# First heads stored and loaded first over two queues, terms interleaved, and the bias fold moved to the last batch

## What is computed

```python
h = _layernorm(x) * (1 + ca) + sa          # sa, ca, ga ... from silu(c) @ wmod
Q, K, V = heads(Wq, bq), heads(Wk, bk), heads(Wv, bv)      # 16 heads of 8
scores = Q K' / sqrt(8) + lambda * (tanh(Q) J) tanh(K)'    # causal
x = x + ga * (softmax(scores) V @ Wo.T + bo)
h = _layernorm(x) * (1 + cb) + sb
expert = argmax(h @ centroids.T)           # 8 experts, one for each row
xn = (h - mu) * rsqrt(var + EPS) * gamma_e + beta_e
y = h + relu(xn @ W1_e.T + b1_e) @ W2_e.T + b2_e
x = x + gb * (alpha * y + (1 - alpha) * h)
```

## Time and profile before

| | |
|---|---|
| median of 3 runs | 775.23 us |
| the profiled execution's own time | 773.26 us |
| its span in the trace | 771.5 us |
| TensorE busy | 676.7 us (88%) |
| VectorE busy | 545.0 us (71%) |
| ScalarE busy | 500.7 us (65%) |
| GpSimd busy | 258.0 us (33%) |

### The profile page before, as it was taken

How to read it: one execution, slowest core, us unless ns; L and a number is a source line. 1 busy time by engine, 2 the same in 40 slices (tenths; PEclk the granted TensorE clock), 3 DMA queues, 4 the chain that set the end, 5 groups by cost and what they waited for, 6 DMA issues and landing times.

```text
span 771.5 us, 15278 instructions
## 1 busy us (share of the span) xinstructions
PE 676.7 (88%) x5199; PEld 341.3 (44%) x5199; DVE 545.0 (71%) x1249; ACT 500.7 (65%) x1182; POOL 258.0 (33%) x342
## 2 busy tenths in 40 slices
PE   3657899999999998999999989999998989887693
PEld 2352344333333433433344434343443227886593
DVE  6959666887866786778667868788777603897352
ACT  1431577766767866766877586866767788655472
POOL 2009109200201943513138234210352202466443
PEclk9867699999999999999999999999999999999797
DMA  8996732456533251925606165636313445424610
GB/s 224 316 206 240 131 68 64 131 98 113 118 67 60 71 178 32 177 56 148 124 1 193 58 112 97 157 94 129 97 43 112 161 142 169 126 78 146 177 40 11
DMA packets 55572, 91.88 MB, mean 119 GB/s; under 512 B 10257, under 2 KB 26157, under 8 KB 55240
## 3 DMA queue, kind: packets, MB, share of 16 engines
q1 hardware_dynamic: 49308, 79.72, 41.6%
q0 software_dynamic: 3520, 8.42, 3.1%
q10 hardware_dynamic: 2668, 2.78, 1.3%
HBM read 51.04 MB, written 37.90 MB: 115 GB/s over the span
## 4 chain that ended last, share of the span: by engine, by line
PE 54%; DVE 20%; ACT 12%; issue 7%; DMA 4%; another core or an unknown queue 1%; ACTq 1%; DVEq 0%; POOL 0%; SPq 0%; POOLq 0%
PE PS L1232 15%; PE PS L1192 12%; PE PS L1258 11%; ACT arenaA L1014 7%; DVE PS L1672 6%; PE PS L1309 4%; PE PS L1320 3%; DVE block_max L1679 3%; ACT arenaB L932 2%; PE PS L1262 2%; DVE arenaA L1355 2%; DVE arenaB L1355 2%; PE PS L1197 1%; PE PS L1140 1%
## 5 line engine op out<-in xcount | busy, mean ns | idle before, releaser
L1014 ACT ACTIVATE arenaA<-PS 128x512 f32<-128x512 f32 (+3 forms) x768 | 332.4, 498 | 157.3 <-PE PS L1262 119.9
L1672 DVE CUSTOM_DVE_ANT_0 PS<-PS,mask 128x1024 f32<-128x1024 f32 (+3 forms) x256 | 261.4, 1035 | 90.4 <-PE PS L1192 85.4
L1258 PE MATMUL PS<-arenaA 99*128 99x512 bf16 (+3 forms) x768 | 221.5, 332 | 14.9 <-ACT arenaA L1014 11.6
L1192 PE MATMUL PS<-arenaA 96*128 96x512 bf16 (+3 forms) x768 | 198.8, 335 | 26.0 <-DVE maxima L1672 8.2
L1258 PEld LDWEIGHTS PS<-arenaA 99*128 99x128 bf16 x768 | 71.6, 97 | 202.5 <-ACT arenaA L1014 141.6
L1232 PE MATMUL PS<-arenaA,Vs 128*9 128x512 f32 (+3 forms) x1536 | 158.3, 488 | 0.0
L1679 DVE TENSOR_REDUCE block_max<-PS 128x8 f32<-128x1024 f32 (+1 forms) x96 | 100.4, 1045 | 28.8 <-PE PS L1197 26.1
L1192 PEld LDWEIGHTS PS<-arenaA 96*128 96x128 bf16 x768 | 66.7, 100 | 90.9 <-DVE maxima L1672 31.3
L1262 PE MATMUL PS<-after,identb 128*128 128x128 bf16 x512 | 104.5, 221 | 0.0
L1063 ACT ACTIVATE arenaA<-PS,b1p 128x128 f32<-128x128 f32 x184 | 52.6, 374 | 35.3 <-PE PS L1309 21.2
L831 POOL DMA_INDIRECT out_dram<-arenaA x46 | 46.1, 1002 | 82.7 <-DVE arenaA L1355 73.8
(11 more groups left out here) (219 smaller groups left out, 691.1 us busy)
## 6 DMA issues: line engine op xcount, KB each, us to landing
arenaA<-k_parts SPq DMA_DIRECT2D x96, 128.0 KB, 8.0
arenaA<-by_expert SPq DMA_DIRECT2D x46, 192.5 KB
o_raw<-OT SPq DMA_DIRECT2D x32, 256.0 KB, 2.1
k_parts<-arenaB SPq DMA_DIRECT2D x24, 256.0 KB, 3.8
arenaA<-q_parts SPq DMA_DIRECT2D x16, 384.0 KB, 5.2
q_parts<-arenaB SPq DMA_DIRECT2D x18, 256.0 KB, 3.8
arenaA<-in_L_ffn_W_dram SPq DMA_DIRECT2D x2, 2048.0 KB, 12.9
arenaA<-q_parts SPq DMA_DIRECT2D x16, 256.0 KB, 5.7
```

The source lines that it names most:

```text
L1014: a.activation(PT[:, u % EB, h, off:HALF], PS[:, 4 + n % SB_, off:HALF], ACT.Exp).then_inc(exp_ok, 1)
L1192: last = mm(PS[:, place + c0 // HALF, at:at + c1 - c0], SQ(g, h)[0:KROWS, t * P:(t + 1) * P], SK(g, h)[0:KROWS, c0:c1], start=(at == 0), s ...
L1258: last = mm(bank[:, off:HALF], SK(g, h)[0:MROWS, kb * P:(kb + 1) * P], SQ(g, h)[0:MROWS, qc * HALF + off:(qc + 1) * HALF], start=True, sto ...
L1672: v.tensor_tensor_reduce(out=src, in0=src, in1=mask[:, S - n:S], scale=1.0, scalar=-3e38, op0=ALU.add, op1=ALU.max, accum_out=maxima[:, pl ...
```

## The change

- **Stores.** `store_first` writes only the first group's 4 heads (64 KB each instead of 256 KB): K's on SyncE, Q's on ScalarE's queue. The other 12 heads (192 KB, all 12 of them on SyncE) follow after the loads of group 0.
- **Loads.** The rows of the six terms become neighbours: row r of term t is now row 6r + t of the stack (`t:KROWS:TERMS`) instead of 16t + r. Queries take 6 transfers of 128 KB as the keys do; a group takes 12 instead of 9. Group 0's queries are issued half by SyncE, half by ScalarE.
- **W2** is loaded after group 0's loads instead of at the start, and its eight turns begin after maximum 13 of group 0 instead of right behind W1's.
- **Order on SyncE.** The values, then a wait for all parts, then group 1; the first maxima are sent between the two stores of turned weights.
- **Fold.** Beta and a second copy of W1 (2 MB in 4 pieces) are loaded in the last body's group 1, into the free part of arena B; b2 with them. GpSimd folds right after its last sends; ScalarE waits for `b1_ok` before `hidden` instead of before attention.

```diff
+            queue.dma_start(stacks[t:KROWS:TERMS, g, side, :, :],
+                            (q_parts, k_parts)[side][bass.ds(b, 1), g * HG:(g + 1) * HG, PART_OF[side][t], :, :].rearrange("a h r q -> (a r) h q"))\
+                .then_inc(stack_in[g], 16)
...
+        FIRST_HEADS = ((0, HG), (HG, H))
+
+        def store_first(queue, n, heads, done):
+
+            k, dst, off = TENSORS[n]
+            h0, h1 = heads
+            for j in range(3):
+                queue.dma_start(dst[0, h0:h1, j, off:off + HD, :], T16[h0 * HD:h1 * HD, k, j, :]).then_inc(done, 16)
...
-            sp.wait_ge(parts0_k, PARTS_OUT // 2)
+                store_first(sp, n, FIRST_HEADS[0], first_k_out)
+            sp.wait_ge(first_k_out, PARTS_OUT // 2)
             load_side(0, 0, 1)
-            sp.wait_ge(parts0_q, PARTS_OUT // 2)
-            load_side(0, 0, 0)
+            sp.wait_ge(first_q_out, PARTS_OUT // 2)
+            for t in (0, 2, 4):
+                load_term(sp, 0, 0, 0, t)
+            sp.dma_start(Aap[:, 20480:24576].rearrange("p (e f) -> p e f", e=E), W2.rearrange("e d n -> d e n")).then_inc(w2_in, 16)
+            for n in (1, 2):
+                store_first(sp, n, FIRST_HEADS[1], parts0_k)
+            for n in (0, 3):
+                store_first(sp, n, FIRST_HEADS[1], parts0_q)
             sp.wait_ge(va_ok, 1)
             load_values(0)
+            sp.wait_ge(parts0_k, PARTS_OUT // 2)
+            sp.wait_ge(parts0_q, PARTS_OUT // 2)
             load_group(0, 1)
...
-            send_maxima(0, T_FIRST)
+                if k == 0:
+                    send_maxima(0, T_FIRST)
...
+                    sp.wait_ge(pv_ok, group * NU + EB + 5 + k)
+                    some = slice(k * E // W_PARTS, (k + 1) * E // W_PARTS)
+                    sp.dma_start(W1F[:, k * E * FC // W_PARTS:(k + 1) * E * FC // W_PARTS, :].rearrange("p (e c) d -> p e (c d)", c=FC),
+                                 W1[some].rearrange("e (p c) d -> p e (c d)", c=FC)).then_inc(fold_in, 16)
+                sp.dma_start(BETA, every(beta)).then_inc(fold_in, 16)
+                sp.dma_start(b2_b[:, :], every(b2)).then_inc(b2_in, 16)
...
+                    if body == "last" and g == 1:
+                        load_fold(b * NG + g)
...
-            pool.wait_ge(b1_ok, 1)
+            pool.wait_ge(b1_in, 16)
...
             send_rows(B - 2, (B - 1) * NG + 2)
+            fold_beta()
...
+                store_first(act, n, FIRST_HEADS[0], first_q_out)
+            act.wait_ge(first_q_out, PARTS_OUT // 2)
+            for t in (1, 3, 5):
+                load_term(act, 0, 0, 0, t)
...
-                for _ in range(6 if i == len(PREP) - 1 else 1 if i >= len(PREP) and turned_weights < 16 else 0):
+                for _ in range(6 if i == len(PREP) - 1 else 1 if i >= len(PREP) + (0 if turned_weights < 8 else W2_FROM) and turned_weights < 16 else 0):
```

More of the change, by code:

```diff
@@ L402, in _ @@
             sp.dma_start(W1r.rearrange("p (e c) d -> p e (c d)", e=E), W1.rearrange("e (p c) d -> p e (c d)", c=FC)).then_inc(w1_in, 16)
-            sp.dma_start(Aap[:, 20480:24576].rearrange("p (e f) -> p e f", e=E), W2.rearrange("e d n -> d e n")).then_inc(w2_in, 16)
-            Q_ROWS = ((0, 0, 3), (3, 0, 2), (5, 0, 1))
-            K_ROWS = ((0, 0, 1), (1, 0, 1), (2, 0, 1), (3, 1, 1), (4, 1, 1), (5, 2, 1))
             def load_side(b, g, side):
-                src, terms = ((q_parts, Q_ROWS), (k_parts, K_ROWS))[side]
-                for t, j, n in terms:
-                    sp.dma_start(stacks[t * ROW:(t + n) * ROW, g, side, :, :],
-                                 src[bass.ds(b, 1), g * HG:(g + 1) * HG, j:j + n, :, :].rearrange("a h j r q -> (a j r) h q"))\
-                        .then_inc(stack_in[g], 16)
+                for t in range(TERMS):
+                    load_term(sp, b, g, side, t)
             def load_group(b, g):
@@ L500, in load_reciprocals, with load_fold @@
                     .then_inc(num_in, 16)
+            def load_fold(group):
+                every = lambda v: v.rearrange("e d -> (e d)").rearrange("(a n) -> a n", a=1).to_broadcast([P, E * D])
+                for g in range(NG):
+                    sp.wait_ge(values_in[g], B * 16)
+                for k in range(W_PARTS):
+                    sp.wait_ge(pv_ok, group * NU + EB + 5 + k)
[4 more added lines that the diff above has]
+                sp.dma_start(b2_b[:, :], every(b2)).then_inc(b2_in, 16)
             def attention(b, body):
@@ L846, in _ @@
             act.dma_start(lam_c[:, :], row(lam).to_broadcast([P, 1])).then_inc(bias_in, 16)
-            act.dma_start(b2_b[:, :], row(b2.rearrange("e d -> (e d)")).to_broadcast([P, E * D])).then_inc(bias_in, 16)
             act.dma_start(b1c[:, :, :], b1.rearrange("e (p c) -> p e c", c=FC)).then_inc(b1_in, 16)
-            act.dma_start(OT[:, :, :].rearrange("p a q -> p (a q)"), row(beta.rearrange("e d -> (e d)")).to_broadcast([P, E * D])).then_inc(beta_in, 16)
             act.wait_ge(cols_ok, 1)
@@ L976, in _ @@
             for n in (0, 3):
-                k, dst, off = TENSORS[n]
                 act.wait_ge(split0_ok, POS0[n] + 1)
-                for j in range(3):
-                    act.dma_start(dst[0, :, j, off:off + HD, :], T16[:, k, j, :]).then_inc(parts0_q, 16)
+                store_first(act, n, FIRST_HEADS[0], first_q_out)
+            act.wait_ge(first_q_out, PARTS_OUT // 2)
+            for t in (1, 3, 5):
+                load_term(act, 0, 0, 0, t)
             for k in range(16):
@@ L1054, in _ @@
             attention(B - 1, "last")
+            act.wait_ge(b1_ok, 1)
             def hidden(n):
@@ L1184, in maximum @@
                 if k == 0:
-                    pe.wait_ge(stack_in[g], (loads + 1) * 9 * 16)
+                    pe.wait_ge(stack_in[g], (loads + 1) * 12 * 16)
                 n = (t + 1) * P
@@ L1793, in _ @@
             last_table = tile_table(1)
+            dve.wait_ge(b2_in, 16)
             for n in range(TURNS):
```

35 lines of the change are left out of this document (18 added, 17 removed).

## The result

The changed kernel takes 776.57 us (median of 16 runs, 773.78 to 778.68), the kernel before beside it on the same chip 774.12 (16 runs). The ratio is 1.003, 95% interval 1.0019 to 1.004: slower by 0.3%, where 770.5 and a gain were predicted. Against the 774.12 measured beside it, the forecast of -4.7 would have been 769.4; it came out at +2.45. One of the 16 runs of the kernel before took 872.41 us, a slow one that the ratio leaves out. The profiled execution took 776.91 us, with a span of 775.1 where it was 771.5.

A forecast was written before the change was run, and what follows sets the result against it. Bound: in setup a chain through Q's last store and group 0's query load, then VectorE. Terms -6.2 + 0 + 0 + 0 + 1.5 = -4.7 from the median of 775.23 gave 770.5 us; range 765.5 to 775.5.

The forecast's parts named there:

- Part 1: Setup, group 0's stacks: first maximum on TensorE moves from 51.78 to 45.6, -6.2 us (bounds -6.6 to +0.3).
- I take 41.3, nearer the low end: Setup: landing time of Q's last first store, chosen between bounds of 40.3 and 45.0 us.
- A quarter of the bytes lands no sooner: Rival, setup: smaller stores on four DMA engines land at 43.9; first maximum -3.6, total -2.1, 773.1 us; chance 0.15.
- ScalarE's "nothing, with 0.2 to spare": Setup: ScalarE's stores and loads before W1's evacuations last to about 42.6; turn 5 ready at 43.3, due 43.5.
- Part 2: Stretch of maxima in setup, W2's eight turns moved behind maximum 13: 0 us (bounds +3.5 to -2.3).
- Half clock at all turns: Rival, stretch of maxima: all eight W2 turns at half clock, +3.5 us, 774; chance 0.05.
- Part 3: Group 1's stack, loaded behind the landed parts, is in by 64 to 67, due at 70.0: 0 us.
- the slower rival: Group 1 late: its loads in at 75 to 78, TensorE waits 5 to 8 us, 777.5 to 779.5; chance 0.08.
- Part 4: Three more transfers per group load, some 21 us of SyncE in all, covered by its waits: 0 us.
- Part 5: Moved fold 0; its loads delay group 14's maxima rows, +1.5 us (bounds 0 to +5).

The follow-up runs named there:

- fold_only: The kernel before with only the change's bias fold (W1 loaded again, beta and b2 in the last body, fold behind the last scatter); ratio 1.0082.
- b2_behind_maxima: The changed kernel with b2's rows alone issued behind group 14's maxima, beta's still ahead of them; ratio to the kernel before 0.9997.
- rows_behind_maxima: The changed kernel with the rows of beta and b2 issued behind group 14's maxima; 768.75 us beside the kernel before's 770.98, ratio 0.9971.
- setup_only: The kernel before with the changes to setup and the row terms, its fold kept at the start; 769.8 us beside 770.98, ratio 0.9986.
- split_without_terms: The kernel before with setup's part of the change, but the stacks' loads in their old form and the old fold; 772.86 us beside 770.82, ratio 1.0021.
- row_terms_only: The kernel before with only the form of the stacks' loads changed (12 per group); 770.69 us, ratio 0.9943; repeated 767.82, 0.9961.
- w2_turned_early: rows_behind_maxima with W2 loaded and turned right behind W1, first maxima sent behind both stores of turned weights; ratio to the kernel before 0.9963.
- terms_and_flat: row_terms_only with the parts reordered in DRAM, all 16 heads in one store of 128 plain rows; ratio to the kernel before 0.9964.
- flat_stores: rows_behind_maxima with the parts reordered in DRAM, so each store is one evenly spaced run of rows; 767.96 us, ratio 0.9913; repeated 764.16, 0.9903.
- flat_split_old_fold: flat_stores with the fold at the start, as in the kernel before; ratio to the kernel before 0.9952; repeated 766.4 us, 0.994.
- store_probe: The changed kernel with eight extra unread stores in the middle bodies; next transfer issued 3.37 and 3.19 us behind 4x8 stores, 3.93 and 3.14 behind 16x8.

## Why the prediction was wrong, by its steps

Two milestones carry most of it. In one table from the profiled executions: VectorE's first maximum, from there to the issue of the first rows, and from the issue of group 14's rows to the evacuation behind it.

| kernel | first maximum | to first rows | at group 14 |
|---|---|---|---|
| before | 52.66 | 27.76 | 10.45 |
| changed, two profiles | 50.55, 51.18 | 29.11, 28.44 | 15.08, 15.72 |
| fold_only | 52.60 | 28.35 | 15.35 |
| b2_behind_maxima | 52.07 | 29.39 | 11.35 |
| rows_behind_maxima | 50.33 | 27.79 | 11.26 |
| setup_only | 51.25 | 29.23 | 10.45 |
| split_without_terms | 53.17 | 28.44 | 10.44 |
| row_terms_only, two | 49.98, 50.39 | 28.80, 27.77 | 10.46, 10.46 |
| w2_turned_early | 49.69 | 28.74 | 10.44 |
| terms_and_flat | 49.32 | 28.81 | 11.25 |
| flat_stores, two | 47.84, 47.55 | 28.45, 28.44 | 10.45, 10.45 |
| flat_split_old_fold, two | 47.84, 47.35 | 26.56, 28.25 | 10.45, 10.45 |

**Part 1, -6.2: measured -2.1, and by another mechanism.** "I take 41.3, nearer the low end" is the step that failed. It let a store shrink with its bytes; the 4x8 pattern kept it at 5.55 us, and the stores landed at 43.62. The two terms behind it were mis-sized as well: the last of three loads was issued 1.5 us later (45.14) where 0.9 was added, and landed in 4.40 where 3.4 was. These are 2.3 + 0.6 + 1.0 of the 4.1 us that were missing. The first is the rival *A quarter of the bytes lands no sooner*, which had the landing right (43.9) but its -3.6 too large by the other two, and got 0.15. I had seen the shape that decides it in the order of instructions. Nor are the 2.1 us due to the stores: row_terms_only gains 2.7 without them (2.3 when repeated), and split_without_terms, with them, is 0.5 later than the kernel before. I had counted the loads' new form only at the end of the path, as 3.4 instead of 5.76 us (4.40 was measured, and 2.62 in row_terms_only), and overlooked that the keys' loads, in the same form, get out of the way of Q's stores.

**ScalarE's "nothing, with 0.2 to spare"**: it hung on the 41.3 and the spare failed with it: ScalarE began 4.65 us later than before, and TensorE stood 2.87. Since the loads landed later still, it cost nothing. In flat_stores, where the stores land at 40.5, ScalarE is at its turns by 42.73 and TensorE doesn't stand, as Part 1 had it.

**Part 2, 0: measured +1.35 and +0.7** in the two profiles. The clock was not full between the first maxima but at 0.50 for 18 us, up to the second of W2's late turns; the other six ran at full clock, so the rival *Half clock at all turns* didn't happen. (Its +3.5 was no exact sum either: 8 turns of 0.4 are 3.2.) Part of the +1.35 is chance, since rows_behind_maxima is the same program up to there and took 27.79, with its clock up at 0.95 between 55 and 60. 1.05 us came back between the first rows and attention's first evacuation. Of these, 0.65 lie before attention's first score products on TensorE, 3.80 us behind the rows' issue before (84.22, after a wait of 0.44 for the rows) and 3.15 here (82.81, after none); the rest isn't traced.

**Part 3, 0**: right. No chunk of group 1 waited for a stack; the slower rival did not happen. (By its own waits of 5 to 8 us it would have ended at 778.5, not 779.5.) **Part 4, 0**: right, and more: the twelve shorter transfers are the one part that gains.

**Part 5, the fold 0, its loads +1.5: measured +4.6.** The mechanism was right, also the slack of nothing, and TensorE's wait of 2.67 us lies in the bounds of 0 to 5. Two things failed. The queueing was mis-sized: the rows landed 6.2 us after their issue, where I had added 1.5 to 3.56, and that 1.5 counts from the end of the issue (580.7 is 2.2 behind its start at 578.50). And the sum had no term for the clock, though the earlier trace rows had shown it fall in setup. Once TensorE stood, the clock fell to 0.50, and the other 1.96 of the 4.6 us were lost behind the wait. In three more profiles with both loads ahead of the rows, waits of 2.62 us (fold_only), 3.37 (store_probe) and 3.78 (the changed kernel again) were followed by a clock of 0.50 and a further 2.3, 1.1 and 1.5 us.

**The sum.** -2.1 + 1.35 - 1.05 - 0.65 (group 12) + 4.63 = +2.2 by the end of attention, and +2.45 in the medians. The range ended at 775.5. The stores' rival (-3.6) with Part 5 at its own bound (+5) gives 775.2 + 1.4 = 776.6. That this is the measured median is luck: the rival's gain was 1.5 too large, and Part 5's bound 0.4. But both losses were in the text, and the range took each alone, while it put only gains together (766.3).

## What to carry to other kernels

Price a DMA by its pattern before its bytes: look at the slowest dimension of both sides of each store, and at how the rows of a load lie over the partitions. A small transfer needed soon must not stand behind a large one that isn't, and moving 1 MB to the other side of it on the same queue was worth 0.5% here. Where an added wait leaves TensorE idle, put the fall of its clock in the sum: 1.1 to 2.3 us behind waits of 2.6 to 3.8 in four profiles of this kernel, none that showed behind 0.84. Work that nobody waits for in the kernel before can come to be waited for once the rest is sooner: the old fold, done at 76 us there, held up attention at 80.7 in flat_split_old_fold.

## What the runs showed that I had not expected

A store of 64 KB in 4x8 rows takes as long to land as one of 256 KB in 16x8 (3.31 and 3.04 us behind the last of three), and the same 64 KB in plain rows half as long (1.74). Its issue is dearer too: 0.58 to 0.70 us where the plain one takes 0.33 to 0.45. Also, the stretch from the first maximum to the first rows varies between 27.8 and 29.4 us for one and the same setup. In the quickest of these the granted clock was back at 0.95 between 55 and 60 us, in the changed kernel's first profile at 0.50 up to 65; the shortest of all, 26.56 in flat_split_old_fold, had 0.96 and 1.00 from 45 to 55 us.
